# A written order for the opening of an attention and mixture-of-experts kernel: x loads, transposes and the zero fill

## The reference

```python
qkv = (x @ w_qkv).reshape(B, S, 3, H, D)            # H = 16 heads of D = 32
q, k = unit_norm(q), unit_norm(k)                   # rope on the even heads
logits = einsum('bshd,bthd->bhst', q, k) * q_gain   # causal, then softmax
x = layernorm(x + (attn @ v) @ w_out)
top_w, top_i = top_k(softmax(x @ gate_w), 2)
routed = sum over the chosen e of top_w * (silu(x @ w_gate[e]) * (x @ w_up[e])) @ w_down[e]
x = layernorm(x + routed + silu(x @ sw_gate) * (x @ sw_up) @ sw_down)
```

## Time and profile before

| | |
|---|---|
| median of 3 runs | 1271.09 us (1271.07 to 1278.27) |
| profiled execution | 1259.98 us |
| its span | 1258.2 us |
| granted TensorE clock, mean | 0.952 |
| TensorE matmul busy | 1135.2 us (90%) |
| VectorE busy | 626.7 us (50%) |
| ScalarE busy | 544.3 us (43%) |
| POOL busy | 520.8 us (41%) |

### The profile page before, as it was taken

The page is one execution under the profiler, slowest core; times in us unless marked ns, Lnnn a source line. Parts: engine busy times, 40 slices in busy tenths (PEclk is TensorE's granted clock), DMA queues, the critical chain, the costliest instruction groups (busy, mean ns, idle before and its releaser), DMA issues.

```text
span 1258.2 us, 19860 instructions
## 1 busy us (share of the span) xinstructions
PE 1135.2 (90%) x6618; PEld 805.7 (64%) x6619; DVE 626.7 (50%) x1120; ACT 544.3 (43%) x894; POOL 520.8 (41%) x376
## 2 busy tenths in 40 slices
PE   5559899998988989998988997998999999998986
PEld 5436355653555535565336886777999999996764
DVE  2424776367661676645755845532222222225775
ACT  2226666566654666556763531111332322221212
POOL 1002454136440364413683303665346464606630
PEclk9769999999988999899998988999999999998988
DMA  5952412334132241323605400655344444316541
GB/s 143 367 151 67 119 34 84 95 91 117 37 88 71 85 117 41 85 68 105 181 1 178 147 1 34 219 201 170 96 140 151 148 145 143 124 48 185 157 136 67
DMA packets 92925, 145.93 MB, mean 116 GB/s; under 512 B 12528, under 2 KB 37104, under 8 KB 92848
## 3 DMA queue, kind: packets, MB, share of 16 engines
q1 hardware_dynamic: 76624, 107.68, 28.2%
q10 hardware_dynamic: 10944, 19.93, 4.6%
q0 software_dynamic: 5280, 17.31, 4.2%
HBM read 86.68 MB, written 58.20 MB: 115 GB/s over the span
## 4 chain that ended last, share of the span: by engine, by line
PE 66%; DVE 15%; issue 6%; POOL 5%; DMA 3%; ACT 3%; SPq 1%; POOLq 0%; ACTq 0%; DVEq 0%
PE scores L500 12%; PE bank L1106 10%; PE scores L1138 7%; PE bank L493 7%; PE scores L557 6%; PE bank L1163 6%; PE bank L595 5%; PE scores L417 3%; PE bank L1160 3%; POOL key_sum L1465 3%; ACT probs L1264 2%; PE scores L515 1%; PE bank L1120 1%; DMA turn_scratch<-turned_l 1%; DVE x L833 1%
## 5 line engine op out<-in xcount | busy, mean ns | idle before, releaser
L1264 ACT ACTIVATE probs<-scores,shift_now 128x1024 f32<-128x1024 f32 (+3 forms) x320 | 299.0, 985 | 132.6 <-PE scores L1138 65.3
L1138 PE MATMUL scores<-q_stack,k_stack 96*128 96x512 f32 (+3 forms) x640 | 205.6, 425 | 21.6 <-DMA k_stack<-turn_scratch 12.8
L1138 PEld LDWEIGHTS scores<-q_stack,k_stack 96*128 96x128 f32 x640 | 116.0, 198 | 156.5 <-issue 76.1
L1465 POOL TENSOR_TENSOR key_sum<-key_sum,probs 128x512 f32<-128x512 f32 (+2 forms) x76 | 154.4, 2032 | 128.9 <-ACT probs L1264 125.2
L1379 DVE TENSOR_TENSOR key_sum<-key_sum,probs 128x1536 f32<-128x1536 f32 (+2 forms) x76 | 157.6, 2074 | 43.7 <-ACT probs L1264 41.8
L1163 PE MATMUL bank<-probs,v_sb 128*32 128x512 f32 (+3 forms) x1280 | 154.6, 556 | 0.0
L500 PE MATMUL scores<-ffn_w,xt_h 128*128 x624 | 131.9, 334 | 4.8 <-issue 4.7
L936 POOL TENSOR_TENSOR ffn_w<-raw,ones 128x1408 fp32r<-128x1408 f32 (+2 forms) x36 | 71.8, 2006 | 147.7 <-PE bank L493 103.5
L500 PEld LDWEIGHTS scores<-ffn_w,xt_h 128*128 128x128 f32 x624 | 103.2, 191 | 14.0 <-issue 11.9
L557 PE MATMUL scores<-x1T_h,ffn_w 128*128 128x512 f32 (+1 forms) x384 | 101.5, 402 | 0.7 <-DVE silu L800 0.7
L940 POOL TENSOR_TENSOR ffn_w<-raw,ffn_w 128x1408 fp32r<-128x1408 f32 (+2 forms) x36 | 91.0, 2539 | 2.1
(11 more groups left out here) (208 smaller groups left out, 1858.8 us busy)
## 6 DMA issues: line engine op xcount, KB each, us to landing
q_stack<-turn_scratch SPq DMA_DIRECT2D x48, 256.0 KB, 3.9
k_stack<-turn_scratch SPq DMA_DIRECT2D x48, 256.0 KB, 3.9
x_sorted<-zeros SPq DMA_DIRECT2D x1, 9984.0 KB, 29.2
y_sorted<-y_tile ACTq DMA_DIRECT2D x39, 256.0 KB, 2.3
x_tile<-x_sorted ACTq DMA_DIRECT2D x37, 256.0 KB, 2.7
turn_scratch<-turned_h SPq DMA_DIRECT2D x32, 256.0 KB, 2.6
turn_scratch<-turned_l SPq DMA_DIRECT2D x32, 256.0 KB, 3.4
raw<-w_gate SPq DMA_DIRECT2D x8, 704.0 KB, 5.4
```

Of the source, the lines that this page charges most:

```text
L1138: mm = nc.tensor.matmul(scores[:, p, hh, lo:CH], k_stack[0:3 * HD, h, j * P:(j + 1) * P], q_stack[0:3 * HD, i % 2, h, lo:CH], start=True, ...
L1264: nc.scalar.activation(probs[:, slot % 4, 2 * p:2 * p + 2, lo:CH], scores[:, p, :, lo:CH], ACT.Exp, bias=shift_now[:, p:p + 1]).then_inc(e ...
L1465: nc.gpsimd.tensor_tensor(key_sum[:, 3, lo:CH], key_sum[:, 3, lo:CH], new, ALU.add).then_inc(sum_pool, 1)
```

## The change

One list, STARTUP, is the order of the opening on TensorE and ScalarE: x tile, projection of chunk 0 or 1, turn of chunk 0. SP loads x tile 0, w_qkv, then the other 15 x tiles with no wait (12 into x_early, 4 into x_late, each with a semaphore), then the tables in one piece each, the gain and the numbers. Twelve tiles are transposed in the opening. Tiles 12 to 15 are transposed in slots 4, 5, 5 and 6 of group 0, through turn_ps, one at a time. POOL splits w before it waits for the tables. The squares of chunk 1 of group 0 get a buffer of their own. The turns of chunk 1 of group 0 move from slot 0 to slots 2 and 3.

In every group, the turns of chunk 3 move from slots 15 and 16 to 18 and 19, those of the next chunk 0 from 31 and 32 to 33 and 34; the projections of the next chunk 1 from 32, 32, 34, 35 to 31 to 34, its norm from 36 and 37 to 35 and 36; the load of w from 18 to 20 and its split from 22 to 23. Slot 15 is added and slot 22 summed directly, which was the other way round.

The zero fill becomes 13 pieces of 3 tiles (786 KB), from a zero tile of 512 B rows, issued by SP in slots 10 to 22 of group 1, each after the scores of the slots before. POOL waits for all 13 before the experts' scatter; ScalarE no longer waits for the fill.

```diff
@@ -58,27 +58,32 @@
 PROJECT_AT = {(2, 0): 1, (2, 1): 2, (2, 2): 3, (2, 3): 4,
               (3, 0): 7, (3, 1): 9, (3, 2): 10, (3, 3): 11,
               (0, 0): 25, (0, 1): 26, (0, 2): 27, (0, 3): 28,
-              (1, 0): 32, (1, 1): 32, (1, 2): 34, (1, 3): 35}
+              (1, 0): 31, (1, 1): 32, (1, 2): 33, (1, 3): 34}
 
 NORMALISE_AT = {(2, 0): 5, (2, 1): 6,
                 (3, 0): 11, (3, 1): 13,
                 (0, 0): 29, (0, 1): 30,
-                (1, 0): 36, (1, 1): 37}
+                (1, 0): 35, (1, 1): 36}
 TURN_AT = {(2, 0): 8, (2, 1): 9,
-           (3, 0): 15, (3, 1): 16,
-           (0, 0): 31, (0, 1): 32,
+           (3, 0): 18, (3, 1): 19,
+           (0, 0): 33, (0, 1): 34,
            (1, 0): 38, (1, 1): 39}
-LOAD_W_AT = 18
-SPLIT_W_AT = 22
+LOAD_W_AT = 20
+SPLIT_W_AT = 23
 SPLIT_WO_AT = 26
 
 
-DIRECT = set(range(STEP_AT[1])) | {4, 5, 6, 10, 11, 14, 15, 23, 28, 29, 30, 36, 38, 39}
+DIRECT = set(range(STEP_AT[1])) | {4, 5, 6, 10, 11, 14, 22, 23, 28, 29, 30, 36, 38, 39}
 ADDING = [i for i in range(NC) if any(n not in DIRECT for n in range(STEP_AT[i], STEP_AT[i + 1]))]
 
-NORM_AFTER = 7
-
-FIRST_AFTER = 5
+FIRST_TURN_AT = (2, 3)
+EARLY = 3 * TPC
+LATE_X_AT = {4: [12], 5: [13, 14], 6: [15]}
+STARTUP = [("x", 0), ("x", 1), ("x", 2), ("p", 0), ("x", 3), ("x", 4), ("p", 1), ("x", 5), ("x", 6), ("p", 2),
+           ("x", 7), ("p", 3), ("x", 8), ("p", 4), ("x", 9), ("p", 5), ("x", 10), ("t", 0), ("t", 1), ("p", 6),
+           ("x", 11), ("p", 7)]
+FILL_TILES = 3
+FILL_AT = range(10, 10 + MAX_TILES // FILL_TILES)
 
 
...
@@ -126,12 +130,14 @@
         wqkv_h = at("wqkv_h", 122880, [P, KC, 3 * P], F32R)
         wqkv_l = at("wqkv_l", 129024, [P, KC, 3 * P], F32R)
         probs = at("probs", 135168, [P, 4, HG, CH], F32)
-        x_in = at("x_in", 135168, [P, 4, D], F32)
+        x_early = at("x_early", 135168, [P, EARLY, D], F32)
+        x_late = at("x_late", 167936, [P, NT - EARLY, D], F32)
         key_sum = at("key_sum", 167936, [P, HG, CH], F32)
...
         qk = [qk_even, qk_odd]
         squares = at("squares", 180224, [P, 2, TPC, HG, HD], F32)
+        squares_second = at("squares_second", 196608, [P, 2, TPC, HG, HD], F32)
         rope_prod = at("rope_prod", 180224, [P, 2, 4, TPC, HG // 2, HD // 2], F32)
         wqkv_raw = at("wqkv_raw", 176128, [P, KC, 3 * P], F32)
         turned_h = at("turned_h", 184320, [P, 2, CH], F32R)
...
@@ -1018,6 +1024,13 @@
 
             return (SLOTS - len(DIRECT)) * g + sum(n not in DIRECT for n in range(slot + 1))
 
+        def x_tile_in(t):
+            return x_early[:, t] if t < EARLY else x_late[:, t - EARLY]
+
+        def xT_bank(t):
+
+            return scores[:, (t % 4) // 2, t % 2, :] if t < EARLY else turn_ps[:]
+
         def load_w(sp, g):
             for part in range(3):
...
@@ -1026,20 +1039,22 @@
 
         @block.sync
         def _(sp):
-            for t in range(NT):
-                if t >= 4:
-                    sp.wait_ge(x_turned, t - 3)
-                sp.dma_start(x_in[:, t % 4, :], x_rows[t * P:(t + 1) * P, :]).then_inc(x_loaded[t % 4], 16)
-                if t == 3:
-                    load_w(sp, 0)
-                    sp.dma_start(tile_numbers[:], numbers.rearrange("(a h) -> a h", a=1).broadcast_to([P, MAX_TILES])).then_inc(numbers_loaded, 16)
-                    for to, of in ((cos, rope_cos), (sin, rope_sin)):
-                        for c in range(NC):
-                            sp.dma_start(to[:, c], of[c * CH:(c + 1) * CH, :].rearrange("(t p) f -> p t f", p=P)).then_inc(tables_loaded, 16)
-                    sp.dma_start(gain[:], q_gain.rearrange("(a h) -> a h", a=1).broadcast_to([P, HEADS])).then_inc(tables_loaded, 16)
-
-            sp.wait_ge(zero_made, 1)
-            sp.dma_start(xs_dram.rearrange("(j p) d -> p j d", p=P), zeros[:].unsqueeze(1).broadcast_to([P, MAX_TILES, D])).then_inc(zero_filled, 16)
+            sp.dma_start(x_early[:, 0], x_rows[0:P, :]).then_inc(x_loaded[0], 16)
+            load_w(sp, 0)
+            for t in range(1, NT):
+                sp.dma_start(x_tile_in(t), x_rows[t * P:(t + 1) * P, :]).then_inc(x_loaded[t], 16)
+            for to, of in ((cos, rope_cos), (sin, rope_sin)):
+                sp.dma_start(to[:].rearrange("p c t f -> p (c t) f"), of.rearrange("(t p) f -> p t f", p=P)).then_inc(tables_loaded, 16)
+            sp.dma_start(gain[:], q_gain.rearrange("(a h) -> a h", a=1).broadcast_to([P, HEADS])).then_inc(tables_loaded, 16)
+            sp.dma_start(tile_numbers[:], numbers.rearrange("(a h) -> a h", a=1).broadcast_to([P, MAX_TILES])).then_inc(numbers_loaded, 16)
+
+            def fill_zeros(part):
+                rows = xs_dram[part * FILL_TILES * P:(part + 1) * FILL_TILES * P, :]
+                if part == 0:
+                    sp.wait_ge(zero_made, 1)
+                sp.dma_start(rows.rearrange("r d -> (r d)").rearrange("(p m n) -> p m n", p=P, n=P),
+                             zeros[:].unsqueeze(1).broadcast_to([P, FILL_TILES * D // P, P])).then_inc(zero_filled, 16)
+
             def stack(g, c, which):
                 C = NC * g + c
                 n = 2 * C + which
...
                         stack(gg, c, which)
                     if slot in STEP_AT and slot:
                         store_y(g, STEP_AT.index(slot) - 1)
+                    if g == 1 and slot in FILL_AT:
+                        sp.wait_ge(scores_ready, 2 * (SLOTS * g + slot))
+                        fill_zeros(FILL_AT.index(slot))
                     if slot == LOAD_W_AT:
                         sp.wait_ge(turned, 2 * (4 * g + 4))
                         if has_following(g):
...
                 nc.tensor.wait_ge(w_high, g + 1)
             if later(g) or c or tt:
                 nc.tensor.wait_ge(qkv_copied, n)
+            if not later(g):
+                nc.tensor.wait_ge(xT_high, TPC * c + tt + 1)
+                nc.tensor.wait_ge(xT_low, TPC * c + tt + 1)
             tok = slice((TPC * c + tt) * P, (TPC * c + tt + 1) * P)
...
@@ -1107,9 +1128,24 @@
                                           start=(m == 0 and k == 0), stop=(m == 2 and k == KC - 1))
             mm.then_inc(qkv_done, 1)
 
+        def pe_turn_x(t):
+
+            nc.tensor.wait_ge(x_loaded[t], 16)
+            if t == EARLY:
+                nc.tensor.wait_ge(turn_low, 4)
+            elif t > EARLY:
+                nc.tensor.wait_ge(xT_low, t)
+            elif t >= 4:
+                nc.tensor.wait_ge(xT_low, t - 3)
+            for k in range(KC):
+                mm = nc.tensor.transpose(xT_bank(t)[:, k * P:(k + 1) * P], x_tile_in(t)[:, k * P:(k + 1) * P], ident[:])
+            mm.then_inc(x_turned, 1)
+
         def pe_turn(g, c, which):
 
             C = NC * g + c
+            if not later(g) and c == 2:
+                nc.tensor.wait_ge(xT_low, NT)
             if which == 0:
                 nc.tensor.wait_ge(q_roped, 2 * (C + 1))
...
@@ -1132,6 +1168,8 @@
             for p in range(2):
                 if later(g) or slot:
                     nc.tensor.wait_ge(exp_done, 2 * n + p - 1)
+                elif p == 0:
+                    nc.tensor.wait_ge(xT_low, EARLY)
                 for hh in range(2):
                     h = 2 * p + hh
                     diagonal = j >= TPC * i
...
+            for kind, n in STARTUP:
+                if kind == "x":
+                    pe_turn_x(n)
+                elif kind == "p":
+                    pe_project(0, n // TPC, n % TPC)
+                else:
+                    pe_turn(0, 0, n)
             def group(g):
                 for slot in range(SLOTS):
                     pe_scores(g, slot)
...
                     for work in work_at(TURN_AT, slot, g):
                         pe_turn(*work)
+                    if not later(g):
+                        for t in LATE_X_AT.get(slot, []):
+                            pe_turn_x(t)
                     if slot or later(g):
                         pe_values(g if slot else g - 1, (slot - 1) % SLOTS)
...
             if later(g) or i >= 2:
                 nc.scalar.wait_ge(y_stored[i % 2], 16 * (NC // 2 * g + i // 2))
+            elif i == 0:
+                nc.scalar.wait_ge(norm_steps, 13 + 1)
             nc.scalar.copy(y_norm[:, i % 2, :], y_ps[:]).then_inc(y_copied, 1)
 
...
-            if not later(g) and slot == 3:
-                nc.scalar.wait_ge(zero_filled, 16)
             if not later(g) and slot == 0:
-                nc.scalar.wait_ge(x_turned, NT)
+                nc.scalar.wait_ge(x_turned, EARLY)
             if later(g) or slot >= 4:
...
+            for t in range(8):
+                dve_x_low(t)
+                if t == 1:
                     dve_split_w(0)
-                if t == NORM_AFTER:
...
+            dve_norms(0, 0)
+            for t in range(8, EARLY):
+                dve_x_low(t)
+                if t % 2:
+                    dve_turn_low(0, 0, t // 2 - 4)
             dve_norms(0, 1)
...
-            pool.wait_ge(tables_loaded, 16 * (2 * NC + 1))
```

(1 more changed line is left out.)

101 lines of the change are left out of this document (43 added, 58 removed).

## The result

The changed kernel takes 1292.96 us (median of 4 runs, 1290.23 to 1293.04), the kernel before 1274.65 with the runs made beside them: ratio 1.0138, 95% interval 1.0096 to 1.0181. It is slower, by 18.3 us or 1.4%; 1276.4 was forecast, 1254 to 1289 as the range. The profiled execution took 1290.23 us.

What follows compares the result with a forecast made beforehand. TensorE carries the chain after an opening held by q and k stores and loads. Terms -13.2 - 2.5 + 4.5 + 15.9 = +4.7, with 0.6 for the clock +5.3: median 1276.4 us, range 1254 to 1289.

Steps and rivals of the forecast that it cites:

- the moved turns: All groups: later turns make w late, 1.5 us lost in each of groups 0, 1, 2; 2.5 gained in group 3.
- the clock: Group 1: a longer fall of the clock in TensorE's wait there, 0.6 us added.
- The opening: Up to the first score: reordered loads and work bring it to 53.0 from 75.27, a gain of 22.3 us.
- Slots 0 to 7: Group 0: q's wait, chunk 1's turns and late x tiles leave 13.2 us of the opening's gain, bounds 9 and 19.
- The fill: Group 1: pieces at 2.7 us each in SP's queue hold up q and w, 15.9 us lost.
- rows 11: Profile rows cited for w's load at 290 to 300 GB/s with queues full, giving 2.7 us a fill piece.
- The order around slots 31 to 35: Each group's end: saves 2.0 us of waits; counted at nothing, between 1 gained and 1.5 lost.
- The fill did not hide: Rival 1, group 1: pieces do not hold up q and w, the 15.9 us go, 1260.5; chance 0.19.
- the turns did not pay: Rival 2: late tiles cost only 2.4 us, each group keeps 3 us of waits, 1254; chance 0.12.
- the order did what it said: Rival 4, opening: early tiles no earlier because x1 waits for w; first score at 57, 1280; within the forecast's 0.57.
- Rival 3: Group 1: small fill elements make pieces slower; at 4 us a piece +17.0, 1288; chance 0.12.
- One sign of being right: Group 1: TensorE waits 10 to 18 us at L1106 for w, not there in groups 0 and 2.

Runs made afterwards that it cites:

- All x in the opening: Changed kernel with late fill, slot tables as before and the last four x tiles also transposed in the opening: 1253.99 us, ratio 0.9851.
- the tiles in other slots: Changed kernel with late fill, slot tables as before and the four late x tiles in slots 0, 1, 4 and 5: 1262.37 us, ratio 0.9917.
- late fill: Changed kernel with the 13 fill pieces in slots 24 to 36 of group 1 instead of 10 to 22: 1279.91 us, ratio 1.0053.
- chunk 3's part alone: Changed kernel with late fill and slot tables as before except around chunk 3: 1283.60 us, ratio 1.0070.
- the early fill: Fill in slots 10 to 22 of group 1: changed kernel 1292.96 us, and the same with all slot tables as before 1277.75 us.
- The run with w first: Changed kernel with late fill and w's load issued ahead of k's stores and stack: 1255.09 us, ratio 0.9863.
- one pair of profiles: Late fill and slot tables as before, with the next chunks' slots moved (1263.16 us) and without (1270.51 us).
- the other: Late fill, all x in the opening, other slots as before, with the next chunks' slots moved (1254.07 us) and without (1253.99 us).
- old slots and late x tiles: Changed kernel with late fill and the slot tables of the kernel before, four x tiles still late: 1270.51 us, ratio 0.9961.

## Why the prediction was wrong

Most of its mechanisms are in the traces; its sum is 10.8 us short of what two profiled executions show (1290.23 less 1274.14 is 16.1; +5.3 was forecast). Two terms were too small: the moved turns (+2.0) and the clock (+0.6).

**The opening.** -22.3 forecast, 75.27 to 53.96 measured: -21.3. **Slots 0 to 7.** 13.2 was to be left, 11.5 is (107.38, 95.84). Wait in slot 4: 3.3 forecast, 2.90; slot 5: 9.0 forecast, 9.8, with the outputs in between as described. All x in the opening took the loss away (9.1 us), the tiles in other slots part of it (3.7).

**The fill.** 15.9 forecast, 13.5 to 13.7 in the profiles and 8 to 11 by the ratios of the medians. 2.7 us a piece was right, and rows 11 were the right rows for it. The price at 2 KB, 2.2 us, was read from issue to landing; at the 400 GB/s at which that fill flows it is 2.0. The rule of the Trainium skill, "DMA: Bandwidth & Descriptors", Specifications, that 512 B is the least size for line rate, is borne out below 512 B (217 GB/s at 256 B, 287 at 512 B), but 512 B did not reach the rate of 2 KB elements here (about 400).

**The moved turns: the step that failed.** "1.5 lost in each of groups 0, 1 and 2; 2.5 gained in group 3", +2.0 in all, with "bounds for all four groups together: 12 gained, 8 lost". The late fill with and without the new slots differs by 9.8 from first score to end and by 9.4 in the medians, and chunk 3's part alone by 13.2: outside the bounds. With the early fill the profiles differ by only 5.1 (624.1, 619.0), the medians by 15.

The chain was the one I gave, q's low half, its stack, k's stack, then w. Its first link was sized too small: "so the low half is 5.4 to 7.3 later, I take 5.8". In group 2, VectorE's adds and q's low half, changed kernel (slot 12 begins at 444.84), then before, run again (431.20):

```profile
457.79 9.07 DVE L1420 TENSOR_TENSOR key_sum<-key_sum,probs 128x1536 f32<-128x1536 f32 x4
466.79 0.68 DVE L1405 TENSOR_TENSOR turned_l<-bank,turned_h 128x512 fp32r<-128x512 f32 x1
```

```profile
443.97 1.76 DVE L1379 TENSOR_TENSOR key_sum<-key_sum,probs 128x1536 f32<-128x1536 f32 x1
445.65 0.68 DVE L1364 TENSOR_TENSOR turned_l<-bank,turned_h 128x512 fp32r<-128x512 f32 x1
```

Counted from the start of slot 12, q's low half begins at 21.95 instead of 14.45: 7.5 later, and 7.7 in group 0. Of the three added adds one lasts 1.76 and two 2.7, where I had put 1.76 to 2.4. From its issue to w's took 9.8 and 11.0 in groups 0 and 2 (10.0 assumed), from there to the split 6.7 and 6.3 (6.9 assumed). So w's low half ends 2.5 and 3.2 later, not 1.6, and slot 26 starts 2.5 and 2.2 to 3.1 later than in the two profiles of before. With the late fill, where new and old slots stand side by side, slots 12 to 25 lose 2.4, 3.7 and 3.1 in the three groups, 9.2 where 4.5 stood, and group 3 gains 1.1, not 2.5. The run with w first shows that the loss comes through this chain: with the same late low half, but w ahead of k's stack, slot 25 takes 4.2 us and no wait for w is left.

The order around slots 31 to 35, counted at nothing, gained 2.0 in one pair of profiles (602.6, 604.5) and lost 3.3 in the other (593.7, 590.4).

**The clock, counted at 0.6.** TensorE's busy time up to the end of attention grew from 578.1 (35.89 + 542.24) to 588.9 (33.42 + 555.48). The x transposes are in both sums, so these 10.8 us are the same work at a lower clock. In slot 38 of group 0 the changed kernel waits 3.18 and then runs slowly:

```profile
212.48 1.11 PE L1156 MATMUL bank<-ident,qk_odd 128*128 128x128 f32 x4 [3.18 <-DVE qk_odd L1400]
213.52 1.51 PE L1201 MATMUL bank<-probs,v_sb 128*32 128x384 f32 x8
```

From the start of that slot to slot 2 of group 1, changed kernel, then before, run again:

```profile
208.10:230.25 22.15, 18.97 (x121) 10.37 (x117) 9.41 (x18) 8.81 (x15) 5.01 (x7) 0.69 0.53 144
220.00:235.24 15.24, 13.34 (x121) 7.96 (x117) 8.18 (x13) 8.56 (x15) 4.80 (x7) 1.00 0.38 122
```

As many matmuls (121) are busy 5.6 us longer, at a clock of 0.69 in place of 1.00, and the wait is 1.3 longer. This is more than all of what group 0 took beyond the forecast: 6.6 more than before (134.41, 127.86), where +1.5 stood. The stretch is 6.9 longer, slots 12 to 25 are 2.5 longer, and slots 26 to 37 2.8 shorter. With the old slots and late x tiles the stretch is 18.13 long at 0.81, with all x in the opening 15.25 at 1.00.

**By group** the misses are 5.1 in group 0, 1.7 in slots 0 to 7, 1.2 in group 1 (18.6 for 17.4), 0.6 in group 2 and 0.2 in group 3: 8.8, less the 0.6 set aside for the clock. The stage behind attention took 2.7 more. The rest of the distance between the medians (16.6 in all, 1292.96 less 1276.4) is the base, 3.1 higher in the second profile (1274.14) than the median that the forecast was added to (1271.09), and the profiled execution, 2.7 below its own median.

**The rivals.** The fill did not hide, the turns did not pay, the order did what it said. Rival 3 had the side right and the time (1288) nearly, but with 4 us for a piece, which is false; that it came near is luck. One sign of being right was wrong as well: no wait for w was to be seen in groups 0 and 2, though the sum itself had w 1.5 late there.

## What to carry to other kernels

When a step is moved later in a queue, follow what is issued behind it to its last user, and ask first whether that user's input was just in time before (w's low half was: TensorE waited 0.2 to 0.3 for it in two groups). One load moved ahead of another turned these slots from 0.5% slower to 1.4% faster than before, and did nothing where the load was not late. Price a stall by the wait and by the busy time behind it: where TensorE is the bound, compare its busy time for the same instructions, and put extra work into a wait that exists already (here 7 us before the first score) rather than into full slots.
